# Lists of the experts' rows made between their products, in both expert-choice stages of a transformer kernel

## The chip, the cores and the metric

One NeuronCore of a Trainium2 chip runs the whole kernel. The metric is the device time of one execution in microseconds (us), lower is better. Engines are named as in the profile: PE (TensorE, matrix products), ACT (ScalarE), DVE (VectorE), POOL (GpSimd), SP (SyncE, which starts plain DMAs). PSUM is the memory that PE writes, SBUF the working memory.

## What is computed

Eight stages follow each other on a residual stream `x` of 16 × 512 tokens with 128 features in float32: attention, feed-forward, attention, feed-forward, and so on. The change concerns the sixth and the eighth stage, which both compute this ("expert choice"): each of 8 experts takes the k rows with the highest probability for it.

```python
x = x + _L1_ffn_ref(_layernorm(x, axis=-1), Ws, bs, W1, b1, W2, b2)

def _L1_ffn_ref(x, Ws, bs, W1, b1, W2, b2):
    B, S, D = x.shape                    # 16, 512, 128
    E = Ws.shape[1]                      # 8 experts, hidden size 512
    N = B * S                            # 8192 rows
    k = int(1.0 * N / E)                 # 1024 rows for each expert
    xf = x.reshape(N, D)
    route_prob = jax.nn.softmax(xf @ Ws + bs, axis=-1).T
    route_vals, routes = jax.lax.top_k(route_prob, k)
    xin = xf[routes]
    h = jax.nn.gelu(jnp.einsum('ekd,edf->ekf', xin, W1) + b1[:, None, :])
    out = jnp.einsum('ekf,efd->ekd', h, W2) + b2[:, None, :]
    out = out * route_vals[..., None]
    final = jnp.zeros((N, D), dtype=x.dtype).at[routes.reshape(-1)].add(out.reshape(-1, D))
    return final.reshape(B, S, D)
```

## The kernel before, in words

`X` lies in SBUF for the whole kernel as 64 tiles of 128 rows (16 blocks `b` of 4 tiles). The stages run one after the other; in every stage each engine has an instruction queue of its own, written out by hand, and waits on semaphores. `feed_forward` makes an expert-choice stage, with tensors named `..._choice_a` for the sixth stage and `..._choice_b` for the eighth. It has three blocks, and all engines meet at the end of each.

1. *Scores.* DVE takes the layernorm statistics of all 64 tiles (L1514, by `statistics`), then block by block normalises `xn` (L1524). PE turns the block (L1476), ACT copies it to `xt` (L1492), PE multiplies it by the router's weights (L1481) and DVE adds the router bias into `gate` (L1534). There is one `xt`, so PE's turn, ACT's copy and PE's product of a block follow each other. SP stores `X` and `xn` to DRAM as rows (`x_rows`, `xn_rows`).
2. *Choice.* Softmax on DVE and ACT. Then 30 steps of bisection on the bits of the probability find each expert's cut: DVE counts the probabilities above a candidate (L1700), PE adds up the counts of an expert's lines (L1580), DVE corrects the candidate in small operations on one column (L1703 to L1706, L1699). Prefix sums give each chosen row its place. Then each expert's list of 1024 row numbers and probabilities is made by a product: `entry` (L1755) holds for each token what the list is to hold, as bfloat16 parts, `onehot` (L1766) its place, 8 tiles at a time in two buffers, and PE multiplies them over 64 tiles into `small` (L1599). DVE takes from `small` the probabilities `prob` and the row numbers `ids` (L1775 to L1780). A loop does this for the 8 experts, and only then the block ends.
3. *Products.* POOL gathers an expert's 1024 rows from `xn_rows` by 8 indirect DMAs of 128 rows each, whose row numbers it reads from SBUF (`idx`, a copy of `ids`, L1931 and L1936). PE turns them (L1967), DVE copies them to `xgT` (L2017), PE multiplies by the first weights (L1979), ACT applies the gelu to `hid` (L2005), PE multiplies by the second weights and adds the bias (L1989, L1991) into `ybank`, DVE scales by `prob` into `yg` (L2023), and POOL adds the rows to `x_rows` by 8 indirect DMAs (L1945). POOL's own queue is: gather expert 0, gather expert 1, and then for each expert e scatter it in two halves, wait until it has landed, and gather expert e+2. At the end SP loads `x_rows` back into `X` (L1923).

The other two feed-forward stages (`pair_feed_forward`, tensors `..._top_a` and `..._top_b`) have their scores in another form, with two `xt` and statistics of 16 tiles at a time; their POOL also starts indirect DMAs (L2338, L2343). They aren't changed.

## Time and profile before

| | us |
|---|---|
| median of 3 runs (lowest, highest) | 6796.9 (6795.12, 6797.51) |
| the profiled execution | 6796.88 |
| its span, first to last instruction | 6795.0 |
| PE busy in the span | 5119.2 (75%) |
| DVE busy | 3765.0 (55%) |
| ACT busy | 3317.2 (49%) |
| POOL busy | 1198.3 (18%) |

The shares are means over eight stages with different limits, so they don't say what bounds the two stages that the change touches; these are to be read by stretches of the timeline. The sixth stage lies at about 3748 to 4335 us of the span and the eighth at about 6192 to 6779 us.

### The profile page before, as it was taken

The numbers are of one execution on the slowest core, as the hardware profiler recorded it, in microseconds if no ns is written. First come the engines' busy times: TensorE is split into PE (matmuls) and PEld (weight loads), VectorE is DVE, ScalarE is ACT, GpSimd is POOL, SyncE is SP. The second block draws the span as 40 slices with busy tenths as digits, with TensorE's granted clock in tenths as the row PEclk, the third lists the DMA queues.
The fourth block names the chain that finished last, engine by engine and source line by source line (L and its number), as shares of the span: only waits on it lengthen the run. The fifth ranks groups of instructions, "written<-read, shape, count | busy, mean of one in ns | idle before, by whom it ended". The sixth has DMA issues, their size and how long they took to land. (4 is left out here: it accounts for less than half of the span.)

```text
span 6795.0 us, 99022 instructions
## 1 busy us (share of the span) xinstructions
PE 5119.2 (75%) x30008; PEld 2655.2 (39%) x30008; DVE 3765.0 (55%) x7864; ACT 3317.2 (49%) x5089; POOL 1198.3 (18%) x1163
## 2 busy tenths in 40 slices
PE   5999619578888709678888347599999999996276
PEld 1333319434444409522222335334343434343244
DVE  4333435477777634566666571266667676755631
ACT  4888416345555315366767002366666666662011
POOL 1000043423333143311110006200000000000035
PEclk9999759789999759789999558799999999997567
DMA  3332511223232501222222103200000000001014
GB/s 82 77 77 75 76 32 50 62 67 89 84 89 85 92 25 51 75 69 60 59 59 54 52 0 53 59 1 0 0 0 0 0 0 0 0 0 52 0 33 91
DMA packets 298528, 310.99 MB, mean 46 GB/s; under 512 B 61526, under 2 KB 249142, under 8 KB 298180
## 3 DMA queue, kind: packets, MB, share of 16 engines
q1 hardware_dynamic: 265756, 269.55, 16.3%
q0 software_dynamic: 32448, 37.39, 2.8%
q8 instruction: 171, 2.80, 0.2%
q14 instruction: 153, 1.25, 0.1%
HBM read 193.61 MB, written 112.80 MB: 45 GB/s over the span
## 5 line engine op out<-in xcount | busy, mean ns | idle before, releaser
L953 ACT ACTIVATE prob_relative<-slot_relative 128x1024 f32<-128x1024 f32 x512 | 499.9, 1042 | 145.9 <-PE obank_relative L827 140.1
L2880 ACT ACTIVATE prob_wide<-slot_wide 128x1024 f32<-128x1024 f32 x512 | 493.8, 1016 | 149.7 <-PE slot_wide L2779 149.7
L1271 DVE TENSOR_TENSOR slot_decay<-slot_decay,dtab_decay 128x512 f32<-128x512 f32 (+3 forms) x1024 | 453.9, 494 | 166.0 <-PE slot_decay L787 146.3
L953 ACT ACTIVATE prob_rms<-slot_rms 128x1024 f32<-128x1024 f32 x512 | 498.0, 1040 | 85.2 <-PE slot_rms L802 83.3
L953 ACT ACTIVATE prob_decay<-slot_decay 128x640 f32<-128x640 f32 x512 | 358.7, 705 | 343.7 <-PE slot_decay L808 342.8
L2779 PE MATMUL slot_wide<-qT_wide,kT_wide 64*128 64x512 f32 x2048 | 508.9, 615 | 2.9 <-ACT prob_wide L2880 2.9
L1283 DVE TENSOR_TENSOR prob_relative<-prob_relative,rtab_relative 128x512 f32<-128x512 f32 (+1 forms) x512 | 409.9, 850 | 128.3 <-ACT prob_relative L953 119.0
L2792 PE MATMUL obank_wide<-prob_wide,v_wide 128*64 128x512 f32 x2048 | 467.7, 599 | 1.8 <-DVE zT_wide L2937 1.8
L1931 POOL COPY idx_choice_b<-ids_choice_b 128x8 int32 (+1 forms) x8 | 1.5, 189 | 2221.9 <-POOLq L1555 2209.9
L827 PE MATMUL obank_relative<-prob_relative,vaug_relative 128*32 128x512 f32 x2048 | 291.4, 644 | 116.7 <-DVE prob_relative L1283 115.0
L2923 DVE TENSOR_TENSOR sums_wide<-sums_wide,prob_wide 128x1024 f32<-128x1024 f32 x256 | 313.7, 1225 | 28.7 <-ACT prob_wide L2880 0.2
L2005 ACT ACT_TABLE_LOAD x8 | 10.3, 1283 | 652.7 <-PE hbank_choice_b L1979 326.4
L802 PE MATMUL slot_relative<-qst_relative,kst_relative 128*128 128x512 bf16 x1024 | 301.5, 393 | 34.4 <-ACT prob_relative L953 28.3
L802 PE MATMUL slot_rms<-qst_rms,kst_rms 128*128 128x512 bf16 x1024 | 283.8, 383 | 34.4 <-DVEq L1263 24.1
L2748 PE MATMUL bench_wide<-wT_wide,xnT_wide 128*128 128x512 f32 x512 | 264.9, 639 | 44.1 <-ACT sq_wide L2838 24.6
L827 PE MATMUL obank_rms<-prob_rms,vaug_rms 128*32 128x512 f32 x2048 | 272.6, 604 | 31.7 <-ACT prob_rms L953 31.6
L2779 PEld LDWEIGHTS slot_wide<-qT_wide,kT_wide 64*128 64x128 f32 x2048 | 176.4, 186 | 287.6 <-issue 280.6
L2853 ACT ACTIVATE rinv_wide<-rbank_wide 128x512 f32<-128x512 f32 x128 | 76.4, 597 | 409.5 <-PE rbank_wide L2803 409.5
L787 PE MATMUL slot_decay<-qst_decay,kin_decay 128*128 128x512 bf16 (+3 forms) x1024 | 229.6, 310 | 60.8 <-issue 41.5
L2792 PEld LDWEIGHTS obank_wide<-prob_wide,v_wide 128*64 128x64 f32 x2048 | 136.0, 137 | 317.8 <-issue 315.2
L802 PE MATMUL slot_decay<-qst_decay,kst_decay 128*128 128x512 bf16 (+3 forms) x1024 | 229.3, 307 | 32.5 <-DVE slot_decay L1271 30.7
L2923 DVE TENSOR_TENSOR sums_wide<-prob_wide 128x1024 f32<-128x1024 f32 x128 | 156.8, 1225 | 174.1 <-ACT prob_wide L2880 174.1
(756 smaller groups left out, 10632.2 us busy)
## 6 DMA issues: line engine op xcount, KB each, us to landing
scratch_decay<-parts_decay SPq DMA_DIRECT2D x192, 128.0 KB, 2.3
qst_rms<-scratch_rms SPq DMA_DIRECT2D x64, 288.0 KB
kst_rms<-scratch_rms SPq DMA_DIRECT2D x192, 96.0 KB
qst_relative<-scratch_relative SPq DMA_DIRECT2D x64, 288.0 KB
kst_relative<-scratch_relative SPq DMA_DIRECT2D x192, 96.0 KB
qst_decay<-scratch_decay SPq DMA_DIRECT2D x128, 128.0 KB
scratch_rms<-parts_rms SPq DMA_DIRECT2D x96, 128.0 KB, 2.3
kst_decay<-scratch_decay SPq DMA_DIRECT2D x192, 64.0 KB
```

What stands on the lines that cost most here:

```text
L787: last = nc.tensor.matmul(slot[:, u % 3, at:at + m], kin[:, h, kb * P:(kb + 1) * P], qst[:, h, q0:S], start=True, stop=False, skip_group_c ...
L802: last = nc.tensor.matmul(slot[:, u % 3, at:at + m], kst[:, h, kb * P:(kb + 1) * P], qst[:, h, q0:S], start=not decay, stop=not decay, ski ...
L827: last = nc.tensor.matmul(obank[32 * j:32 * j + 32, c0:c1], vaug[:, vp, kb, G * g + j, :], prob[:, Q % 2, j, at + c0 - q0:at + c1 - q0], s ...
L953: nc.scalar.activation(prob[:, Q % 2, j, 0:c1 - c0], slot[:, u % 3, c0:c1], ACT.Exp).then_inc(exp_done, 1)
L1271: last = nc.vector.tensor_tensor(sl, sl, dtab[:, h, 0:m], ALU.mult)
L1283: last = nc.vector.tensor_tensor(v, v, rtab[:, h:h + 2, c0:c0 + (hi - lo) * P], ALU.mult)
L2748: nc.tensor.matmul(bench[:, j % 2, :], xnT[:, t * P:(t + 1) * P], wT[:, j // 2, (j % 2) * S:(j % 2 + 1) * S], start=True, stop=True).then_ ...
L2779: last = nc.tensor.matmul(slot[:, u % 2, hh * S:(hh + 1) * S], kT[r, Q, kb * P:(kb + 1) * P], qT[r, Q, :], start=True, stop=True)
L2792: nc.tensor.matmul(obank[W * hh:W * hh + W, :], v[:, kb, (2 * Q + hh) * W:(2 * Q + hh + 1) * W], prob[:, Q % 2, kb, hh * S:(hh + 1) * S], ...
L2853: nc.scalar.activation(rinv[:], rbank[:], ACT.Ln).then_inc(r_logged, 1)
L2880: nc.scalar.activation(prob[:, Q % 2, u % 4, :], slot[:, u % 2, :], ACT.Exp).then_inc(exp_done, 1)
L2923: add = nc.vector.tensor_tensor(sums[:, Q % 2, :], first, prob[:, Q % 2, i + 1, :], ALU.add)
```

## The change

`model` calls a new function, `choice_feed_forward`, for the sixth and the eighth stage. It computes the same, in one block instead of three:

- Scores in the form of `pair_feed_forward`: statistics of 16 tiles at a time, all of `xn` kept, two `xt`, PE's product of block b−1 after the turn of block b.
- The bisection is written out 30 times without a loop, with three small operations on DVE instead of five.
- `row`, `lane` and the count constants are bfloat16, `fact` holds its five parts side by side, and `entry` is made for one expert at a time (two buffers). `onehot` holds 64 tiles in one buffer. DVE runs `mark(e)` (one `in_lane`, five `entry`, eight `onehot`) and `read(e)` for e = 0 to 7 as fast as its waits let it. PE makes lists 0 and 1 ahead of the products, and list e+2 between the first and the second product of expert e.
- ACT copies the turned rows and scales by `prob`, both of which DVE did.
- POOL reads `ids` directly, without the copy `idx`, and waits for the landing of scatter e−1 before scatter e instead of behind it.
- SP loads the weights of expert e when those of e−2 are used; `X` is loaded back by four DMAs instead of one.

```diff
+def choice_feed_forward(nc, sem, A, X, NB, w, uid):
...
+            @block.gpsimd
+            def _(pool):
+                def gather(e):
+                    pool.wait_ge(list_read, e + 1)
+                    if e >= 2:
+                        pool.wait_ge(xg_turned, 2 * (e - 1))
+                    for j in range(JT):
+                        nc.gpsimd.indirect_dma_start(
+                            xg[:, e % 2, j, :], None, xn_rows,
+                            bass.IndirectOffsetOnAxis(ap=ids[:, e, j:j + 1], axis=0)).then_inc(gathered[e % 2], 16)
+
+                def scatter(e):
+                    if e:
+                        pool.wait_ge(scattered, 16 * JT * e)
+                    for half in range(2):
+                        pool.wait_ge(yg_ready, 2 * e + half + 1)
+                        for j in range(HALF * half, HALF * (half + 1)):
+                            nc.gpsimd.indirect_dma_start(
+                                x_rows, bass.IndirectOffsetOnAxis(ap=ids[:, e, j:j + 1], axis=0),
+                                yg[:, e % 2, j, :], None, compute_op=ALU.add).then_inc(scattered, 16)
...
+                gather(0)
+                gather(1)
+                for e in range(E):
+                    scatter(e)
+                    if e + 2 < E:
+                        gather(e + 2)
...
+                def make_list(e):
+                    pe.wait_ge(entries, e + 1)
+                    if e >= 2:
+                        pe.wait_ge(list_read, e - 1)
+                    for i in range(T):
+                        if i % 8 == 0:
+                            pe.wait_ge(hot_ready, e * (T // 8) + i // 8 + 1)
+                        last = nc.tensor.matmul(small[:, 64 * (e % 2):64 * (e % 2) + LIST], onehot[:, i, :],
+                                                entry[:, e % 2, i, :], start=(i == 0), stop=(i == T - 1),
+                                                skip_group_check=True)
+                        if i % 8 == 7:
+                            last.then_inc(list_filled, 1)
...
+                    if e + 2 < E:
+                        make_list(e + 2)
...
+                    act.wait_ge(list_read, e + 1)
+                    for half in range(2):
+                        act.wait_ge(y_filled, 2 * e + half + 1)
+                        if e >= 2:
+                            act.wait_ge(scattered, 16 * JT * (e - 1))
+                        for j in range(HALF):
+                            at = HALF * half + j
+                            last = nc.scalar.activation(yg[:, u, at, :], ybank[:, half, j * D:(j + 1) * D], ACT.Copy,
+                                                        scale=prob[:, e, at:at + 1])
+                        last.then_inc(yg_ready, 1)
...
+                for i in range(BITS):
+                    nc.vector.tensor_scalar(work2[:], gate2[:], cand[R].bitcast(F32), None, ALU.is_ge, ALU.add,
+                                            accum_out=col[R, 0:1]).then_inc(counted, 1)
+                    dve.wait_ge(summed, i + 1)
+                    link(nc.vector.tensor_scalar(bit[R], small[R, 0:1], float(KEEP), float(1 << (BITS - 1 - i)),
+                                                 ALU.is_ge, ALU.mult))
+                    link(nc.vector.tensor_tensor(cur[R], cur[R], bit[R], ALU.bitwise_or))
+                    if i + 1 < BITS:
+                        link(nc.vector.tensor_scalar(cand[R], cur[R], 1 << (BITS - 2 - i), None, ALU.bitwise_or))
...
+                def mark(e):
+                    if e >= 2:
+                        dve.wait_ge(list_filled, (e - 1) * (T // 8))
+                    link(nc.vector.tensor_tensor(in_lane[:, e % 2], lane[:, e, :].unsqueeze(2).to_broadcast([P, T, JT]),
+                                                 lanes, ALU.is_equal))
+                    for k in range(FACTS):
+                        last = nc.vector.tensor_tensor(entry[:, e % 2, :, k * JT:(k + 1) * JT], in_lane[:, e % 2],
+                                                       fact[:, e, :, k].unsqueeze(2).to_broadcast([P, T, JT]), ALU.mult)
+                    last.then_inc(entries, 1)
+                    for g in range(T // 8):
+                        if e:
+                            dve.wait_ge(list_filled, (e - 1) * (T // 8) + g + 1)
+                        nc.vector.tensor_tensor(onehot[:, 8 * g:8 * g + 8, :], countb[:].unsqueeze(1).to_broadcast([P, 8, P]),
+                                                row[:, e, 8 * g:8 * g + 8].unsqueeze(2).to_broadcast([P, 8, P]),
+                                                ALU.is_equal).then_inc(hot_ready, 1)
...
+                mark(0)
+                read(0)
+                for e in range(1, E):
+                    mark(e)
+                    read(e)
...
-            lambda: feed_forward(nc, sem, A, X, "choice", NB, dict(
+            lambda: choice_feed_forward(nc, sem, A, X, NB, dict(
```

In the order of instructions, PE's queue of the changed kernel stands like this where the products begin; the first row is the lists of experts 0 and 1, and the rest is expert 0 up to the first of its second products.

```order
L2753 MATMUL small_choice_a<-entry_choice_a,onehot_choice_a 128x40 x128
L2768 MATMUL bench_choice_a<-ident_choice_a,xg_choice_a 128x128 x8
L2779 MATMUL hbank_choice_a<-xgT_choice_a,up_choice_a 128x512 x8
L2753 MATMUL small_choice_a<-entry_choice_a,onehot_choice_a 128x40 x64
L2792 MATMUL ybank_choice_a<-down_choice_a,hid_choice_a 128x128 x4
```

The 64 products of a list, which all stood ahead of the products before, now lie between an expert's first products (`hbank`) and its second (`ybank`).

On DVE, before, the entries of all experts were made at once and the lists by a loop in the block ahead of the products:

```order
L1755 TENSOR_TENSOR entry_choice_a<-in_lane_choice_a,fact_choice_a 128x512x8 x5
L1758 UNCONDITIONAL_BRANCH
L1758 ISA
L1766 ISA
L1766 TENSOR_TENSOR onehot_choice_a<-count_choice_a,row_choice_a 128x1024
```

Now the same queue holds, for each expert, this run (`part`, `row` and `ids` belong to `read`, the rest to `mark`):

```order
L2930 TENSOR_TENSOR in_lane_choice_a<-lane_choice_a,countb_choice_a 128x512
L2933 TENSOR_TENSOR entry_choice_a<-in_lane_choice_a,fact_choice_a 128x64x8 x5
L2939 TENSOR_TENSOR onehot_choice_a<-countb_choice_a,row_choice_a 128x1024 x8
L2947 COPY part_choice_a<-small_choice_a 128x8
L2948 TENSOR_TENSOR part_choice_a<-part_choice_a,small_choice_a 128x8
```

Fourteen operations with two inputs in SBUF follow each other for each expert, and nothing else of DVE's stands in the products any more. On POOL the loop is gone and the queue begins so:

```order
L2675 DMA xg_choice_a<-xn_rows_choice_a,ids_choice_a 128x128 x16
L2685 DMA x_rows_choice_a<-yg_choice_a,ids_choice_a 8192x128 x8
L2675 DMA xg_choice_a<-xn_rows_choice_a,ids_choice_a 128x128 x8
L2685 DMA x_rows_choice_a<-yg_choice_a,ids_choice_a 8192x128 x8
```

The sixteen gathers, the eight scatters of an expert and the eight gathers of the next but one follow each other as before; what is gone is the copy of the row numbers between them.

## Rows read from the trace of the kernel before

**Rows 1.** The sixth stage by stretches, all engines; the columns head the rows.

```profile
core 0: us, PE busy (x) PEld busy (x) DVE busy (x) ACT busy (x) POOL busy (x), PEclk, DMA share, GB/s
...
3844.00:3929.00 85.00, 17.56 (x60) 15.00 (x60) 46.35 (x211) 0.00 (x0) 0.00 (x0) 0.50 0.00 0
...
3954.00:3976.00 22.00, 0.00 (x0) 0.00 (x0) 21.97 (x6) 0.00 (x0) 0.00 (x0) 0.50 0.00 0
...
3976.00:4082.00 106.00, 69.90 (x512) 53.31 (x512) 81.61 (x105) 0.00 (x0) 0.17 (x1) 0.50 0.00 0
...
4082.00:4317.00 235.00, 176.88 (x832) 120.14 (x832) 29.98 (x88) 48.52 (x68) 163.00 (x136) 0.85 0.33 54
```

**Rows 2.** Timeline, scores of the fourth and the sixth stage (start, busy, idle before).

```profile
2316.01 3.18 DVE L183 BATCH_NORM_STATS2 stats_top_b<-X 128x6 f32<-128x128 f32 x16
...
2384.52 0.19 DVE L2378 TENSOR_TENSOR gate_top_b<-ybank_top_b,rb_top_b 128x32 f32<-128x32 f32 x1 [1.51 <-PE ybank_top_b L2182]
...
3756.22 12.46 DVE L183 BATCH_NORM_STATS2 stats_choice_a<-X 128x6 f32<-128x128 f32 x64
...
3836.86 0.69 DVE L1684 TENSOR_REDUCE tok_choice_a<-gate_choice_a 128x64 f32<-128x512 f32 x1 [0.62 <-PEq L1433]
```

**Rows 3.** Timeline of the bisection: its first memset, then one step.

```profile
3843.04 0.48 DVE L1693 MEMSET ones_choice_a<- 128x512 f32 x1 [0.17 <-DVE gate_choice_a L1630]
...
3903.79 0.75 DVE L1700 TENSOR_SCALAR_CACHE_REDUCE work_choice_a<-gate_choice_a,colT_choice_a 128x512 f32<-128x512 f32 x1
...
3905.23 0.16 DVE L1703 TENSOR_SCALAR colT_choice_a<-small_choice_a 128x1 int32<-128x1 f32 x1 [0.68 <-PE small_choice_a L1580]
...
3906.63 0.75 DVE L1700 TENSOR_SCALAR_CACHE_REDUCE work_choice_a<-gate_choice_a,colT_choice_a 128x512 f32<-128x512 f32 x1
```

**Rows 4.** Groups by line: count, busy us, mean ns, idle before.

```profile
L1755 DVE TENSOR_TENSOR entry_choice_a<-in_lane_choice_a,fact_choice_a 128x4096 bf16<-128x4096 bf16 x5 | 21.8, 4421 | 0.0
...
L1746 DVE TENSOR_TENSOR in_lane_choice_a<-lane_choice_a,count_choice_a 128x4096 bf16<-128x4096 f32 x1 | 4.4, 4426 | 0.0
...
L1766 DVE TENSOR_TENSOR onehot_choice_a<-count_choice_a,row_choice_a 128x1024 bf16<-128x1024 f32 x64 | 75.7, 1223 | 9.1 <-PE small_choice_a L1599 5.9 <-issue 3.2
...
L1599 PE MATMUL small_choice_a<-entry_choice_a,onehot_choice_a 128*128 x512 | 69.9, 212 | 67.8 <-DVE onehot_choice_a L1766 66.3 <-issue 0.2
...
L2305 ACT ACTIVATE part_top_a<-ybank_top_a,xg_top_a 128x128 f32<-128x128 f32 x91 | 33.4, 368 | 28.2 <-PE ybank_top_a L2250 28.2
```

**Rows 5.** Timeline of POOL from one expert's gathers to the next one's.

```profile
4130.37 0.19 POOL L1931 COPY idx_choice_a<-ids_choice_a 128x8 int32 x1 [2.00 <-DMA x_rows_choice_a<-yg_choice_a,idx_choice_a]
...
4135.30 0.95 POOL L1936 DMA_INDIRECT xg_choice_a<-xn_rows_choice_a,idx_choice_a  x1 [0.30 <-issue]
...
4154.72 1.56 POOL L1945 DMA_INDIRECT x_rows_choice_a<-yg_choice_a,idx_choice_a  x1 [0.30 <-issue]
...
4158.38 0.19 POOL L1931 COPY idx_choice_a<-ids_choice_a 128x8 int32 x1 [2.10 <-DMA x_rows_choice_a<-yg_choice_a,idx_choice_a]
```

**Rows 6.** Timeline of PE in the products of one expert.

```profile
4117.48 0.66 PE L1967 MATMUL bench_choice_a<-ident_choice_a,xg_choice_a 128*128 128x128 f32 x4
...
4120.04 7.03 PE L1979 MATMUL hbank_choice_a<-xgT_choice_a,up_choice_a 128*128 128x512 f32 x16
...
4138.41 0.48 PE L1991 MATMUL ybank_choice_a<-b_choice_a,ones_choice_a 1*128 x2
```

**Rows 7.** Timeline of DVE and POOL in the fourth stage, around its scatter.

```profile
2454.69 2.79 DVE L2483 TENSOR_TENSOR owner_top_b<-held_top_b,count_top_b 1x2548 f32<-1x2548 f32 x1
...
2455.59 2.78 POOL L2338 DMA_INDIRECT xg_rows_top_b<-xng_top_b,spots_top_b  x1 [210.04 <-DVE spots_top_b L2481]
...
2461.47 0.97 POOL L2338 DMA_INDIRECT xg_rows_top_b<-xng_top_b,spots_top_b  x1 [0.31 <-issue]
...
2463.87 8.88 DVE L2493 TENSOR_TENSOR X<-X,xng_top_b 128x2048 f32<-128x2048 f32 x4
...
2464.01 10.25 POOL L2338 DMA_INDIRECT xg_rows_top_b<-xng_top_b,spots_top_b  x1 [0.30 <-issue]
```

311 lines of the change are left out of this document (310 added, 1 removed).

## The prediction

> **What bounds the kernel now.** I read the sixth stage by windows first [rows 1], then the timelines inside each window, then the groups by line. In the windows the reader is to see a chain of stretches with a different owner each: 85 us of bisection in which DVE and PE are both under 55% busy, so that latencies set its pace; 22 us in which DVE alone makes the entries; 106 us of lists, DVE busy 81.6 of them; and 235 us of products, of which PE is busy 176.9 and POOL 163.0. No stretch overlaps the next. In the products the period of an expert is 28.0 us (4130.37 to 4158.38 [rows 5]), and it is POOL's: eight gathers of 0.95 + 0.30, eight scatters of 1.56 + 0.30, a copy, and some 2 us of waiting for the landing. PE needs 21.4 us for an expert (4117.48 to 4138.89 [rows 6]) and waits the rest. The eighth stage has the same form, and I count it as a second sixth.
>
> **The change part by part.** The sum is made against the profiled execution, 6796.88 us, which is also the median. All terms are for one stage.
>
> *Scores.* The new form is that of the fourth stage, which runs from its first statistics to its last `gate` in 68.7 us (2316.01 to 2384.71 [rows 2]); the sixth takes 80.0 (3756.22 to 3836.24). Taken: −11.3. No gain is excluded by the row itself; between 0 and −13.
>
> *Ends of blocks, setup.* One block boundary goes (0.62 [rows 2]) and memsets of about 0.48 move to where DVE waits for loads [rows 3]: −2.0, between −0.6 and −2.5.
>
> *Bisection.* A step takes 2.84 us (3903.79 to 3906.63 [rows 3]): 1.44 up to the first correction, then small operations and the loop's branch. With three operations of 0.16 + 0.03 a step is 1.44 + 0.57 = 2.01. Thirty steps fall from 84.7 (a little under 85.2) to 60.3: −24.4, between −18 (a step of 2.2) and −27.
>
> *Placing.* `in_lane` for all experts, 4.4 us [rows 4], leaves this phase; a copy and part of a wait for the second turn go, and the five strided writes of `fact` may each cost 0.2 more. Estimate −5.6, between −4 and −7. The parts so far come to 43.3.
>
> *Lists and products.* Before, from the first entry (3954) to the end of the products (4317) [rows 1] it is 363 us. For after I count from the start of `mark(0)`.
>
> DVE's run for one list: five entries an eighth as long as 4421 ns [rows 4], 0.55 + 0.06 each, 3.1 in all; `in_lane` 0.7; eight `onehot` of 1024 elements at the entries' 1.08 ns each, 1.11 + 0.03, so 9.1 (they took 1223 ns). Together 12.9. Behind it PE's last group takes 1.1 (69.9 us / 64 [rows 4]) and `read` about 1.1: list 0 is read at 15.2, the run of list 1 lies at 15.2 to 28.1, that of list 2 at 30.4 to 43.3. PE per expert: 21.4 + a list, 4.6 at the full clock (an estimate, half of 69.9/8 = 8.7 and a little) = 26.2. POOL per expert: 8 × 1.86 + 8 × 1.25 = 24.9. ACT's four scalings of 0.37 [rows 4] put 1.5 us between a half's products and its scatter; they and its two copies fit beside its 48.5 us of 235.
>
> What decides is whether POOL keeps its 24.9 when DVE runs lists beside it, which it never does in the products of before. The nearest case stands in [rows 7]. A DVE operation with both inputs in SBUF runs 2454.69 to 2457.48; POOL's indirect DMA begun at 2455.59 takes 2.78 and ends 0.89 behind it, where one beside other work takes 0.97. Four such operations follow each other for 8.88 us from 2463.87; the DMA begun at 2464.01 takes 10.25, to 2474.26. It did not get in between the four. Each of the fourteen operations of a list is of that kind. So I take it that a run holds up POOL from its start to its end, except that one DMA gets through behind `in_lane`, where the next operation waits for it. A run then costs POOL 12.9 − 1.5 = 11.4 us. The rule of the Trainium skill that bears on it ("SBUF — State Buffer", "SBUF: two separate sides") is that VectorE and GpSimd share an exclusive pair of ports which the one that starts first holds for its whole instruction, and a VectorE operation with two SBUF inputs takes it against a GpSimd one that reads SBUF. The first part agrees with the 2.78; but release at every instruction's end would have let POOL in between the four, and the 10.25 speaks against that. What it would be by the rule stands as a rival below.
>
> With that the stage runs so: gather 0 starts at 15.3, gets one DMA through behind `in_lane`, two between the runs, one more in the next run, and its last four behind 43.3: it ends at 48.3. PE starts at 50.3 (2.0 of landing, as [rows 5] show for the scatter). The first scatter starts 24.1 later, at 74.4: turn and first products 9.6 [rows 6] and 2.4 for a clock that has gone low in the wait, list 4.6, half of the second products 6.0, scaling 1.5. Then follow: a first period of 42.8 (24.9, the rest of the run of list 3, 6.5, and all of list 4's, 11.4); three of 24.9 + 11.4 = 36.4, for the runs of lists 5, 6 and 7; two without a run, 26.1 and 25.1; a scatter with its landing, 18.2, and the last, 17.2. The end is at 74.4 + 42.8 + 109.2 + 51.2 + 18.2 + 17.2 = 313. Against 363: −50. With a list on PE at the low clock (8.7) it is 317; with `onehot` at 1.22 and dearer ends of the held DMAs 321; the least is 308.
>
> The wait for scatter e−1 moved ahead of scatter e is free: the gathers lie between. SP's loads and the four-part load of `X` are left at nothing; the same bytes move.
>
> *Sum.* −11.3 − 2.0 − 24.4 − 5.6 − 50 = −93.3 for a stage, −187 for both: 6796.9 − 187 = **6610 us**. With each term at its bound it is 6575 to 6650, and taken together more likely 6590 to 6635.
>
> **The rivals.**
>
> *POOL gets in between operations.* For it: the 2.78 alone would read so. Against: the 10.25. If at every second boundary one DMA gets in, a run costs about 6 us, gather 0 ends at 32.3, and the first scatter starts at 58.4. Periods are 33.9, three of 31, then as above: 58.4 + 33.9 + 93 + 51.2 + 35.4 = 272, −91, a stage −134.3, both −269: 6528 us. This is also what the Trainium skill's rule would give.
>
> *POOL isn't held up at all.* For it: operands here are bfloat16 with repeated elements, those of [rows 7] were float32. Then PE sets the pace: it starts at 29.2, the first scatter at 51.4, and 51.4 + 5 × 26.2 + 25.1 + 35.4 = 243, −120, both stages −327: 6470 us.
>
> *Slower: PE's clock stays low.* The granted clock was 0.50 (1.2 GHz) through bisection and lists and 0.85 over the products [rows 1], where PE waits 6.6 us of 28.0. With waits of 10 us of 36.4 it may fall each time. If it stayed at 0.50 throughout, PE's work of an expert is 176.88/8 × 0.85/0.50 = 37.6, the list 8.7, pauses inside 3.7: 50 us. The end is at 50.3 + 6 × 50 + 2 × 41.3 + 11.3 = 444, +81, a stage +38: 6872 us. It decides from 45 us for an expert on. Against: PE would then be busy nearly without a pause, and in such work the clock did rise.
>
> *Dearer for POOL.* Each DMA under a run might hold up DVE in turn, or waits chain so that lists come late to PE. 330 or more for the part, 6650 or more in all.
>
> **How the numbers follow.** The forecast 0.66, POOL in between 0.15, POOL free 0.12, slower 0.03, dearer but still faster 0.04. The predicted time is the first's. The range takes it whole with its dear side and the second rival: 6515 to 6650; POOL free, the slower case and what lies above are left out. The forecast's own range is 6590 to 6635. 0.2% (14 us) is about what a measurement of this kernel can tell from no change. Faster 0.96: every case but the slower one and its like; within 0.2% 0.01; slower 0.03.
>
> **What would show it.** Scores of 68 to 69 us; bisection steps of 2.0; in each list's run one POOL DMA of 9 to 12 us that ends just behind the last `onehot`; scatter 1, 2 and 3 starting 36 us apart; PE waiting some 10 us for gathers of most experts. The forecast is wrong if POOL's DMAs beside `onehot` take 1 us (then 6470), or 2 to 3 us each (then 6528); if PE's turn follows the gathers by a clock of 0.50 through whole experts; or if `onehot` or `entry` take a length other than 1.1 and 0.6, which changes every run by eight or five times that. It is also wrong if DVE makes the lists later than PE wants them.

## The result

| | us |
|---|---|
| before, median | 6796.5 |
| after, median of 4 runs (lowest, highest) | 6510.5 (6506.6, 6514.9) |
| after / before, 95% interval | 0.9579 (0.9567, 0.9591) |
| span before, after | 6795.0, 6505.7 |

The change makes the kernel 286 us faster. The forecast was 187 us (6610 us), with a range down to 6515: the direction was right, and the time lies below the range. The stretches of the sixth stage in the changed kernel, as in [rows 1] (a view by windows; the columns head it):

```profile
core 0: us, PE busy (x) PEld busy (x) DVE busy (x) ACT busy (x) POOL busy (x), PEclk, DMA share, GB/s
3757.00:3826.00 69.00, 40.20 (x192) 39.49 (x192) 48.06 (x270) 9.38 (x16) 0.00 (x0) 0.50 0.48 138
3832.00:3892.00 60.00, 17.54 (x60) 14.97 (x60) 36.56 (x150) 0.00 (x0) 0.00 (x0) 0.50 0.00 0
3913.00:4175.00 262.00, 193.39 (x1344) 134.71 (x1344) 109.33 (x153) 72.64 (x145) 192.12 (x128) 0.83 0.29 45
```

The reader is to see that scores (69 us), bisection (60) and the rest are still separate stretches, but that lists and products are now one of 262 us, in which PE is busy 193 us and POOL 192. Beside the stretches of before this gives, for the sixth stage:

| part | before | after | difference | forecast |
|---|---|---|---|---|
| scores | 80.0 | 68.7 | −11.3 | −11.3 |
| setup, softmax and block end | | | −1.0 | −2.0 |
| bisection, 30 steps | 84.7 | 60.0 | −24.7 | −24.4 |
| placing | 25.4 | 21.3 | −4.1 | −5.6 |
| first entry to last landing | 363.0 | 261.6 | −101.4 | −50 |

The sum is −142.5, and the next stage begins 142.7 us earlier. So four of the five terms were right within 1.5 us, and for one the forecast was half of what came. DVE's timeline of the changed kernel, one step of the bisection, beside [rows 3]:

```profile
3847.95 0.74 DVE L2881 TENSOR_SCALAR_CACHE_REDUCE work_choice_a<-gate_choice_a,cand_choice_a 128x512 f32<-128x512 f32 x1
...
3849.96 0.75 DVE L2881 TENSOR_SCALAR_CACHE_REDUCE work_choice_a<-gate_choice_a,cand_choice_a 128x512 f32<-128x512 f32 x1
```

From one count to the next it is 2.01 us, as worked out ahead.

What the missing term consists of is seen on POOL and DVE. Below are two gathers of expert 0 and the first scatter, then the first scatters of experts 1 to 4, and last DVE's run of `onehot` beside the first of them (start, busy, idle before):

```profile
3935.85 1.96 POOL L2675 DMA_INDIRECT xg_choice_a<-xn_rows_choice_a,ids_choice_a  x1 [0.30 <-issue]
...
3940.39 0.95 POOL L2675 DMA_INDIRECT xg_choice_a<-xn_rows_choice_a,ids_choice_a  x1 [0.30 <-issue]
...
3964.99 7.90 POOL L2685 DMA_INDIRECT x_rows_choice_a<-yg_choice_a,ids_choice_a  x1 [8.09 <-ACT yg_choice_a L2829]
...
4000.29 1.62 POOL L2685 DMA_INDIRECT x_rows_choice_a<-yg_choice_a,ids_choice_a  x1 [0.30 <-issue]
...
4029.20 1.62 POOL L2685 DMA_INDIRECT x_rows_choice_a<-yg_choice_a,ids_choice_a  x1 [0.30 <-issue]
...
4058.83 1.62 POOL L2685 DMA_INDIRECT x_rows_choice_a<-yg_choice_a,ids_choice_a  x1 [0.30 <-issue]
...
4087.43 1.62 POOL L2685 DMA_INDIRECT x_rows_choice_a<-yg_choice_a,ids_choice_a  x1 [0.30 <-issue]
```

```profile
3931.24 9.16 DVE L2939 TENSOR_TENSOR onehot_choice_a<-countb_choice_a,row_choice_a 128x1024 bf16<-128x1024 bf16 x8
...
3962.22 9.16 DVE L2939 TENSOR_TENSOR onehot_choice_a<-countb_choice_a,row_choice_a 128x1024 bf16<-128x1024 bf16 x8
```

Beside the run that begins at 3931.24, each gather takes 1.97 us and starts 2.27 after the one before it: two operations of 1.14. Behind the run it takes 0.95. So POOL gets in between DVE's operations, which the sum of the forecast had ruled out. Gather 0 ends 29.4 us after the first mark at 3913.19 (forecast 48.3), the first scatter starts at 51.8 (74.4), and the scatters of experts 1 to 4 begin 28.6 to 29.6 us apart (36.4). Only one DMA of each stage is held in the way that was forecast: in this one the scatter of 3964.99 takes 7.90 us, to 1.5 us behind the end of the run that began at 3962.22.

PE in an expert of the changed kernel (compare [rows 6]):

```profile
4013.58 1.78 PE L2753 MATMUL small_choice_a<-entry_choice_a,onehot_choice_a 128*128 128x40 bf16 x64
...
4031.27 1.11 PE L2768 MATMUL bench_choice_a<-ident_choice_a,xg_choice_a 128*128 128x128 f32 x4 [4.00 <-DMA xg_choice_a<-xn_rows_choice_a,ids_choice_a]
```

The list, 64 products, takes 1.78 us at the full clock and not the 4.6 of the estimate. PE waits some 4 us for the gathers of most experts (9 once), and turn and part of the first products then run at the low clock, but it is up again before the second products.

### The profile page after: what moved, and what is told of

Same layout as the page of the kernel before. It is cut to its first block and busy times, and to the rows that moved or that the text cites. A ratio compares the mean times of both kernels' runs of the same rounds, so it can differ in the third digit from the quotient of the medians.

```text
span 6505.7 us, 95125 instructions
## 1 busy us (share of the span) xinstructions
PE 4965.4 (76%) x29755; PEld 2574.5 (40%) x30008; DVE 3701.5 (57%) x7740; ACT 3366.0 (52%) x5243; POOL 1256.0 (19%) x1147
## 5 line engine op out<-in xcount | busy, mean ns | idle before, releaser
L2675 POOL DMA_INDIRECT xg_choice_b<-xn_rows_choice_b,ids_choice_b x64 | 85.4, 1334 | 2072.6 <-DVE ids_choice_b L2951 2053.4
L802 PE MATMUL slot_relative<-qst_relative,kst_relative 128*128 128x512 bf16 x946 | 281.0, 390 | 50.3 <-ACT prob_relative L953 35.7
L802 PE MATMUL slot_rms<-qst_rms,kst_rms 128*128 128x512 bf16 x945 | 268.6, 382 | 42.2 <-issue 24.7
L787 PE MATMUL slot_decay<-qst_decay,kin_decay 128*128 128x128 bf16 (+3 forms) x960 | 214.0, 303 | 69.6 <-issue 41.8
L3354 DVE TENSOR_TENSOR rfix_wide<-rbank_wide,rinv_wide 128x512 f32<-128x512 f32 x128 | 88.5, 692 | 247.2 <-ACT rinv_wide L3275 247.2
```

Of the source, the lines that this page charges most:

```text
L787: last = nc.tensor.matmul(slot[:, u % 3, at:at + m], kin[:, h, kb * P:(kb + 1) * P], qst[:, h, q0:S], start=True, stop=False, skip_group_c ...
L802: last = nc.tensor.matmul(slot[:, u % 3, at:at + m], kst[:, h, kb * P:(kb + 1) * P], qst[:, h, q0:S], start=not decay, stop=not decay, ski ...
L2675: nc.gpsimd.indirect_dma_start(xg[:, e % 2, j, :], None, xn_rows, bass.IndirectOffsetOnAxis(ap=ids[:, e, j:j + 1], axis=0)).then_inc(gathe ...
```

## The experiments

The theories after the result. **A**: POOL's DMA needs what a two-input DVE operation holds once, and gets it at the end of an operation. **B**: gathers get in, scatters don't. **C**: the first DMA after a pause is held. **D**: two inputs have nothing to do with it. Times of the variants are given as their ratio to the runs of before on the same chip, times 6796.5.

### The cost by itself: probe

A kernel of its own, in which nothing of the model is computed: DVE runs operations of one kind while POOL issues 8 indirect DMAs. Its figures, and those of the other small kernels below, are of one execution.

```python
ARMS = [("gather", "none", 0), ("scatter", "none", 0), ("store", "none", 0),
        ("gather", "onehot", 14), ("scatter", "onehot", 14), ("store", "onehot", 14),
        ("gather", "entry", 24), ("scatter", "entry", 24),
        ("gather", "wide", 7), ("scatter", "wide", 7),
        ("gather", "scalar", 64), ("scatter", "scalar", 64),
        ("gather", "psum", 14), ("scatter", "psum", 14),
        ("gather", "onehot_late", 14), ("scatter", "onehot_late", 14)]
```

> Nothing of the model is computed here: sixteen arms one after the other, each 8 indirect DMAs of 128 rows on POOL (gather from DRAM, scatter with addition, or plain store) beside a run of DVE operations (none; onehot of 128x1024 bfloat16 with two SBUF inputs; entry of 128x512; 128x2048 float32 of 2.2 us; onehot for one tile at a time with one SBUF input; onehot with one input in PSUM; onehot begun when the first DMA has landed). Theory A (every boundary between DVE operations is a chance, whatever the DMA): beside onehot a gather and a scatter both take about 2.3 us with their gap, beside the 2.2 us operations about 4.5 or 2.2. Theory B (the kind of DMA decides): gathers beside onehot take 2.0 us each, but the first scatter is held to the end of the run, some 14 us, and so is a plain store or not, which tells whether the addition or the SBUF source matters. Theory C (the first DMA after a pause is held, whatever its kind): the first gather beside onehot takes some 14 us, and in the arms begun late no scatter does. Theory D (nothing to do with two inputs in SBUF): the arms with one SBUF input or a PSUM input look like those with two. With A, B or C those arms show 0.95 for a gather and 1.55 for a scatter.

POOL's timeline, a DMA out of the middle of an arm: gather and scatter beside `onehot`; gather beside 128x2048 operations, beside one-input operations, and beside those with an input in PSUM:

```profile
84.61 1.97 POOL L307 DMA_INDIRECT xg_probe<-x_rows_probe,ids_probe  x1 [0.30 <-issue]
...
103.69 1.97 POOL L309 DMA_INDIRECT x_rows_probe<-xg_probe,ids_probe  x1 [0.31 <-issue]
...
175.50 1.90 POOL L307 DMA_INDIRECT xg_probe<-x_rows_probe,ids_probe  x1 [0.30 <-issue]
...
208.57 0.94 POOL L307 DMA_INDIRECT xg_probe<-x_rows_probe,ids_probe  x1 [0.30 <-issue]
...
239.74 0.94 POOL L307 DMA_INDIRECT xg_probe<-x_rows_probe,ids_probe  x1 [0.30 <-issue]
```

| beside | gather | scatter | store |
|---|---|---|---|
| nothing | 0.94 | 1.54 | 0.96 |
| `onehot`, 1.14 us | 1.97 | 1.97 | 1.97 |
| entries, 0.61 us: the first three | 1.3 to 1.5 | 1.9 to 2.1 | |
| entries: the last five | 0.94 | 1.54 | |
| 2048 columns float32, 2.2 us | 1.90 | 1.90 | |
| one SBUF input, 0.16 us | 0.94 to 0.99 | 1.55 | |
| one input in PSUM, 1.14 us | 0.94 | 1.54 to 1.62 | |

A DMA waits for the next end of an operation and ends 0.9 us (gather) or 1.5 us (scatter) behind it. With the gap of 0.30, gathers and scatters beside `onehot` start 2.27 us apart, two operations of 1.14, and beside the long ones 2.20, one operation of 2.2. Beside entries the fourth gather began within 0.01 us of an operation's start and got through at once, and so did those behind it. A holds, B falls (scatters get in as gathers do), C falls (no first DMA was held), and D falls: with one input, or one of the two in PSUM, nothing is lost. This is the rule of the Trainium skill ("SBUF — State Buffer", "SBUF: two separate sides") as it was cited ahead, and for DVE's side the trace agrees, with release at the end of each instruction. For POOL's side it doesn't: by the rule a DMA that comes first would hold DVE up for its whole 0.94 us, but beside entries the operation behind such a start followed after 0.65 us and not 0.60. So POOL holds up DVE for some 0.05 us only.

### Does a certain place in an operation hold the DMA: probe_phase

Also a kernel of its own. An ACT copy of growing width starts two DMAs at ten places in an operation of the run, about 0.16 us apart.

> Nothing of the model is computed here. Twenty arms: a run of twelve onehot operations on DVE (1.14 us each), and two indirect DMAs on POOL after a pause, begun at ten places about 0.1 us apart within an operation; ten arms with gathers, ten with scatters. In the changed kernel the first scatter of a stage was issued 0.48 us after such an operation had begun and took 7.9 us, to the end of the run. Theory of the place: a DMA issued near that place in an operation misses all boundaries; so one or two of the ten scatters take some 9 us, the others 1.6 to 2.7, and perhaps so for the gathers. Theory of bad luck by kind or of another cause (what POOL did before, or the waits between the operations): no DMA here takes more than 2.7 us, and all end about 0.9 us (gather) or 1.5 us (scatter) behind a boundary.

```profile
39.82 2.14 POOL L271 DMA_INDIRECT xg_probe<-x_rows_probe,ids_probe  x1 [39.38 <-ACT line_probe L261]
...
137.08 0.94 POOL L271 DMA_INDIRECT xg_probe<-x_rows_probe,ids_probe  x1 [10.54 <-ACT line_probe L261]
...
191.16 2.52 POOL L273 DMA_INDIRECT x_rows_probe<-xg_probe,ids_probe  x1 [10.08 <-ACT line_probe L261]
```

The first gather takes 2.14, 1.91, and so on down to 0.94, where an operation's end is just reached, and then 1.92 again; the first scatter 1.55 to 2.52. It is a wait for the next end, whatever the place, and none of the 20 first DMAs was held longer. So the place alone doesn't explain the 7.90.

### Lists ahead of the products: lists_ahead

```diff
-                make_list(0)
-                make_list(1)
+                for e in range(E):
+                    make_list(e)
...
-                    if e + 2 < E:
-                        make_list(e + 2)
```

> All eight lists ahead of the products again, the rest as changed. If DVE's runs are what lengthens POOL's period (29.0 us for an expert against 24.9 by its own durations), the period is 25 us here: the lists end 8 x 14.3 = 114 us after the first mark, the first scatter starts at about 135, six periods of 25 and 35 for the last two scatters end at 320, against 262 now: 59 us more for a stage, 6629 us in all. If something else in the changed stage makes the 29.0, it stays, and the time is 6680 us.

Measured: ratio 0.9747 (0.9731, 0.9764), 6625 us, where 6629 was expected. Gathers of successive experts on POOL:

```profile
4137.23 1.01 POOL L2675 DMA_INDIRECT xg_choice_a<-xn_rows_choice_a,ids_choice_a  x1 [0.30 <-issue]
...
4162.32 1.01 POOL L2675 DMA_INDIRECT xg_choice_a<-xn_rows_choice_a,ids_choice_a  x1 [0.30 <-issue]
```

The period is 25.1 us, so the 4 us by which it was longer are DVE's runs. Of the 286 us, the interleaving is worth 115 (6625 − 6510); the rest is in the other edits.

### One SBUF input: one_input

```diff
-        row = sb("row", [P, E, T], BF16)
+        row = sb("row", [P, E, T])
...
-                        nc.vector.tensor_tensor(onehot[:, 8 * g:8 * g + 8, :], countb[:].unsqueeze(1).to_broadcast([P, 8, P]),
-                                                row[:, e, 8 * g:8 * g + 8].unsqueeze(2).to_broadcast([P, 8, P]),
-                                                ALU.is_equal).then_inc(hot_ready, 1)
+                        for i in range(8 * g, 8 * g + 8):
+                            last = nc.vector.tensor_scalar(onehot[:, i, :], countb[:], row[:, e, i:i + 1], None,
+                                                           ALU.is_equal)
+                        last.then_inc(hot_ready, 1)
```

> onehot is made one tile at a time by an operation with one SBUF input and a value for each partition; entries are as before. Theories A, B and C, in which two SBUF inputs take the port that POOL needs: gathers beside onehot fall from 1.97 to 0.95 us, gather 0 ends after 10 us, the period is POOL's own 25 us, and the part from the first mark to the last landing falls from 262 to about 234 us: 6455 us in all. Theory D: the gathers beside onehot stay at 1.97, and the time stays at 6510 us. If 64 small operations take DVE much longer than the 9.2 us of the 8 (over 0.3 us each), lists come late and the gain is lost: 6510 to 6560 us.

Measured: 0.9740 (0.9707, 0.9773), 6620 us, 110 us slower than the changed kernel, a miss by 165. The gathers did what was expected:

```profile
3933.70 0.96 POOL L2675 DMA_INDIRECT xg_choice_a<-xn_rows_choice_a,ids_choice_a  x1 [0.30 <-issue]
...
3968.47 1.63 POOL L2685 DMA_INDIRECT x_rows_choice_a<-yg_choice_a,ids_choice_a  x1 [15.47 <-ACT yg_choice_a L2829]
...
4008.38 1.62 POOL L2685 DMA_INDIRECT x_rows_choice_a<-yg_choice_a,ids_choice_a  x1 [11.85 <-ACT yg_choice_a L2829]
```

0.96 us, but the scatters then wait 12 to 15 us for `yg`. Behind that stands PE. By a window of one expert, and PE's timeline of the list and what follows:

```profile
core 0: us, PE busy (x) PEld busy (x) DVE busy (x) ACT busy (x) POOL busy (x), PEclk, DMA share, GB/s
...
3968.00:4008.00 40.00, 35.54 (x173) 26.00 (x172) 14.29 (x71) 9.04 (x19) 20.17 (x16) 0.63 0.25 40
```

```profile
3988.62 1.81 PE L2753 MATMUL small_choice_a<-entry_choice_a,onehot_choice_a 128*128 128x40 bf16 x53
...
3992.35 0.27 PE L2753 MATMUL small_choice_a<-entry_choice_a,onehot_choice_a 128*128 128x40 bf16 x4 [0.53 <-issue]
3993.79 0.23 PE L2753 MATMUL small_choice_a<-entry_choice_a,onehot_choice_a 128*128 128x40 bf16 x2 [1.17 <-issue]
...
3998.12 2.06 PE L2792 MATMUL ybank_choice_a<-down_choice_a,hid_choice_a 128*128 128x128 f32 x8 [0.16 <-issue]
```

An expert takes 40 us, PE is busy 35.5 of them, and the granted clock is 0.63. The list ends in gaps of 0.5 to 1.2 us that no engine releases, and behind them eight second products take 2.06 to 2.08 us and not 1.16: the low of the two clock levels (1.2 GHz). DVE stood idle beside these gaps (from 3972.83 to 3998.37), so its small operations don't make them. This is the forecast's slower rival, PE at a low clock for most of an expert (there 50 us), and it came in a variant that was to be faster. What it needs is not POOL's hold but a list in which PE stands still.

### Runs beside scatters: beside_scatter

The landing of an expert's first scatter gets a semaphore of its own, and DVE waits for it.

```diff
+                    if e >= 3:
+                        dve.wait_ge(began, 16 * (e - 2))
                     link(nc.vector.tensor_tensor(in_lane[:, e % 2], ...
```

> DVE begins the run of list e (from e = 3) only when the first of the scatters of expert e-3 has landed, so that it lies beside scatters and not beside gathers. Theory B (a scatter is held through the whole run): one scatter of each expert takes some 12 us, 7 us more than the gathers lose now, five times in a stage: 6580 us. Theory A: scatters get in between operations, lose 0.4 us each, and the time falls to about 6490 us. Theory C: POOL doesn't pause there, so no scatter is held: as A.

Measured: 0.9651 (0.9635, 0.9667), 6559 us, near the 6580 of theory B, and B is false all the same:

```profile
3975.20 1.97 POOL L2688 DMA_INDIRECT x_rows_choice_a<-yg_choice_a,ids_choice_a  x1 [0.31 <-issue]
...
4029.29 1.62 POOL L2688 DMA_INDIRECT x_rows_choice_a<-yg_choice_a,ids_choice_a  x1 [10.43 <-ACT yg_choice_a L2834]
...
4039.62 1.75 POOL L2688 DMA_INDIRECT x_rows_choice_a<-yg_choice_a,ids_choice_a  x1 [2.85 <-ACT yg_choice_a L2834]
...
4121.45 8.26 POOL L2688 DMA_INDIRECT x_rows_choice_a<-yg_choice_a,ids_choice_a  x1 [2.63 <-ACT yg_choice_a L2834]
```

```profile
core 0: us, PE busy (x) PEld busy (x) DVE busy (x) ACT busy (x) POOL busy (x), PEclk, DMA share, GB/s
...
4029.00:4071.00 42.00, 36.55 (x171) 25.95 (x169) 13.69 (x19) 8.85 (x18) 21.45 (x16) 0.62 0.23 38
```

Scatters beside the run take 1.97 as gathers do. The time went where it went in one_input: 42 us for an expert at a clock of 0.62, after lists that had gaps. A list that waited for DVE for 1.25 us in all left the clock up. One scatter of each stage was held here as well, 8.26 us (4121.45) and 7.50. It is the first after a pause, but so is that of 4039.62, beside the same kind of run, with 1.75 us.

### The list in eight portions: two_spread and one_spread

```diff
                             last = nc.tensor.matmul(y, ones[0:1, 0:P], b2[:, e * D:(e + 1) * D], start=False,
                                                     stop=True, skip_group_check=True)
-                        last.then_inc(y_filled, 1)
+                            if j == HALF - 1:
+                                last.then_inc(y_filled, 1)
+                            if e + 2 < E:
+                                make_list(e + 2, [HALF * half + j])
```

one_spread has this with the one-input `onehot`, two_spread with the changed kernel's.

> The changed kernel, but the 64 products of list e+2 lie in eight portions between the eight groups of the second products of expert e. POOL sets the period (29.0 us, 4.1 of it beside onehot), so PE's order shouldn't matter by itself; DVE's run begins up to 12 us later and lies beside scatters, which lose 0.4 us each and not 1.0: some 1.7 us an expert less, 10 a stage: 6490 us. If the clock of PE falls less, PE's wait is longer and nothing is gained by it. If the list read later delays gather e+2, 6510 to 6530 us.

> onehot with one SBUF input as in the run one_input, and the list in eight portions as in two_spread. One_input took 40 us for an expert, all of them PE's, with PE's clock at 0.62 and stretches within the list in which PE stood still. Theory F or G, the stop or the weak work of the list brings the clock down: spread out it doesn't, PE takes 23.5 us, POOL 24.9 sets the period, and the part from the first mark to the last landing is about 235 us: 6455 us in all. If it is something else about the 512 small operations of DVE (their instructions, or the time they take) that slows PE, it stays near 6620 us.

Measured: two_spread 0.9540 (0.9524, 0.9556), 6484 us; one_spread 0.9514 (0.9499, 0.9530), 6466 us. Both expectations hold within 0.2% (6490 and 6455). one_spread on POOL, the first scatters of two experts, and by windows:

```profile
3988.43 1.62 POOL L2685 DMA_INDIRECT x_rows_choice_a<-yg_choice_a,ids_choice_a  x1 [0.30 <-issue]
...
4013.90 1.62 POOL L2685 DMA_INDIRECT x_rows_choice_a<-yg_choice_a,ids_choice_a  x1 [0.30 <-issue]
```

```profile
core 0: us, PE busy (x) PEld busy (x) DVE busy (x) ACT busy (x) POOL busy (x), PEclk, DMA share, GB/s
...
4000.00:4029.00 29.00, 25.62 (x188) 18.18 (x186) 21.73 (x115) 9.65 (x19) 23.73 (x18) 0.88 0.39 60
4029.00:4059.00 30.00, 29.08 (x252) 22.12 (x249) 15.60 (x77) 9.99 (x22) 23.91 (x21) 1.00 0.38 62
```

The period is 25.5 us, POOL's own 24.9 and a little, at a clock of 0.88 to 1.00. One_input and one_spread differ only in where the 64 products stand: 154 us. The share of the two-input `onehot` alone is the difference of two_spread and one_spread, 18 us by the ratios, whose intervals overlap slightly. It is clear of noise all the same: both ran on one chip, and there the four times of each (6478 to 6489 and 6465 to 6469 us) stand apart, with medians 14 us from each other. one_spread is the fastest version here, 44 us below the changed kernel.

### What stops PE in the list: probe_fetch, probe_far and one_hold

The gaps in one_input and beside_scatter stood in lists beside which POOL gathered; a list beside scatters had none. The theory (F) was that PE's instructions come late beside gathers.

> Nothing of the model is computed here. Arms on PE: 16 products of 128x512 in float32, then 64 small bfloat16 products as in a list, then 40 products of 128x128 in float32; beside them 16 indirect DMAs of POOL (gather, scatter, store), eight plain DMAs, or nothing; in two arms the small ones are spread over the last 40, in one PE pauses for some 4 us behind the list. Theory F (PE's instructions come late beside gathers): the list takes 1.8 us beside nothing and 4 us or more beside gathers, with idle stretches that no engine releases; scatters or plain DMAs may do it too. Theory G (the list itself, short products, makes PE's clock fall): no gaps anywhere, and the last 40 products fall to the low clock in all arms but the spread ones. Behind gaps of 2 us in all I expect the last 40 products at the low clock (0.26 us each) for some us, else 0.14.

> Nothing of the model is computed here. As in probe_fetch, no gap came into a list of 64 beside any DMA; but the rows gathered there lay in order, and the gaps in the runs one_input and beside_scatter began after some 48 small products. So here the list is 256 small products and the rows lie 61 rows apart (one arm has them in order). Theory F2 (PE's instructions come late beside gathers, seen only when what is fetched ahead is used up): 256 products take 6.8 us beside nothing, and 15 us or more beside gathers, in gaps of 0.5 to 1.2 us, and the clock falls behind them. If 256 take 6.8 us in all arms, gathers alone don't do it. If they gap beside nothing too, the rate of PE's instructions alone limits a long list.

Both are kernels of their own. PE's timeline beside gathers, of 64 products in order of rows, and of 256 with rows far apart, each with the products of 128x128 behind them:

```profile
88.54 1.78 PE L290 MATMUL small_probe<-entry_probe,hot_probe 128*128 128x40 bf16 x64
90.17 9.18 PE L307 MATMUL ybank_probe<-X,wt_probe 128*128 128x128 f32 x80
```

```profile
96.61 6.66 PE L290 MATMUL small_probe<-entry_probe,hot_probe 128*128 128x40 bf16 x256
103.12 9.18 PE L307 MATMUL ybank_probe<-X,wt_probe 128*128 128x128 f32 x80
```

The list takes 1.78 us beside gathers and beside nothing, and 256 take 6.66 in all arms; the 80 records behind them take 9.18 at the full clock. F falls in this form, and so does G, that such a list brings down the clock by itself. In the arm with a pause of 3.69 us ahead of them they took 10.82.

So the same was asked in the kernel. one_hold is one_input with one more wait on POOL:

```diff
                     pool.wait_ge(list_read, e + 1)
+                    if 2 <= e < E - 1:
+                        pool.wait_ge(list_filled, (e + 2) * (T // 8))
```

> As one_input, but gather e waits until list e+1 is complete, so that no gather runs while PE makes a list; nothing else is changed. Theory F2: the list has no gaps, PE keeps its clock in the second products, an expert takes 25 to 28 us and not 40, and the time falls from 6642 to about 6480 us although POOL has more to wait for. Rival (the list as one block brings the clock down by itself, or the 512 small operations of DVE do): gaps or the low clock stay, and so do 40 us for an expert and 6620 to 6660 us.

Measured: 0.9555 (0.9539, 0.9571), 6494 us, 126 below one_input, where 6480 was expected. The first two rows are of the list that is made before the held gathers begin and of what follows it; the other two are lists with the gathers held:

```profile
3957.57 0.37 PE L2755 MATMUL small_choice_a<-entry_choice_a,onehot_choice_a 128*128 128x40 bf16 x8 [0.93 <-DVE onehot_choice_a L2942]
...
3963.16 2.08 PE L2794 MATMUL ybank_choice_a<-down_choice_a,hid_choice_a 128*128 128x128 f32 x8
...
4016.06 1.78 PE L2755 MATMUL small_choice_a<-entry_choice_a,onehot_choice_a 128*128 128x40 bf16 x64
...
4045.73 1.78 PE L2755 MATMUL small_choice_a<-entry_choice_a,onehot_choice_a 128*128 128x40 bf16 x64
```

```profile
core 0: us, PE busy (x) PEld busy (x) DVE busy (x) ACT busy (x) POOL busy (x), PEclk, DMA share, GB/s
...
3996.00:4022.00 26.00, 24.38 (x188) 17.88 (x188) 17.79 (x81) 8.95 (x18) 21.12 (x17) 1.00 0.37 62
4022.00:4050.00 28.00, 23.42 (x159) 15.73 (x158) 13.53 (x73) 8.95 (x18) 20.86 (x18) 0.82 0.35 57
```

With no gather beside it the list takes 1.78 us without a gap, an expert 26 to 28 us, and the clock is 0.82 to 1.00. So within this stage it is the gathers beside the list that stop PE. That the stop brings the clock down, whoever makes it, is seen in the first of these lists: it waits for DVE three times for 0.93 us, and the second products behind it take 2.08 us as in one_input. By themselves, in small programs, gathers and a list don't make gaps, and neither do gathers beside the portions of eight in one_spread. What else is needed, whether the other transfers or the length of the program, stays open.

## Why the prediction was wrong

- *Scores, ends of blocks, bisection, placing*: right, −41.1 together against −43.3. The memsets that were moved did not vanish behind a load (0.9 us), and the five strided writes of `fact` took 0.88 us each and not 0.43, where 0.2 more was allowed. The bounds of the terms, as they stand, add up to 6588 and 6668 us and not to 6575 and 6650; the measured time is below both.
- *POOL held up by a run*: this is the step that failed: "So I take it that a run holds up POOL from its start to its end". It rested on one row, the 10.25 us of [rows 7]. Probe, probe_phase and the changed kernel show in its place that a DMA waits for the next end of an operation, costing about 1 us for a gather beside `onehot`, 0.4 for a scatter, and little beside entries. An expert lost 4 us and not 11.4. In the stage the forecast was 22.6 us too late with the first scatter and 29.6 too long in the four periods behind it, and 0.8 too short at the end: together the 51.4 us that the term is off. Not all of the 22.6 is POOL's: gather 0 ends 18.9 us sooner, and of the other 3.7 the list on PE is 2.8 (1.78 us and not 4.6).
- The trace of before had a row against this step, between those that [rows 7] show:

```profile
2457.52 2.80 DVE L2485 TENSOR_TENSOR owner_top_b<-owner_top_b,pairs_top_b 1x2548 f32<-1x2548 f32 x1
...
2458.68 2.48 POOL L2338 DMA_INDIRECT xg_rows_top_b<-xng_top_b,spots_top_b  x1 [0.30 <-issue]
```

  The DMA begun at 2455.59 [rows 7] ended at 2458.38, when the next operation with two inputs had begun at 2457.52: it got in between the two. The DMA behind it ended 0.84 us behind the end of that second operation. Two DMAs followed the right mechanism and one, the 10.25, didn't.
- The rival *POOL gets in between operations*, 6528 us, was the right mechanism, with the pitch of one DMA for two operations. It was 18 us too slow, since it let entries cost as much as `onehot` and took the list for 4.6 us; that it came so near is in part luck, since it had no DMA held for the rest of a run, 6 us a stage the other way. It had a chance of 0.15: the 2.78 of [rows 7] spoke for it, and one row against it was given too much weight.
- *POOL isn't held up at all*: wrong, but its bound was reached by one_spread, 6466 us against 6470.
- *PE's clock stays low*: not so in the changed kernel, where from the second expert on a list falls beside scatters, because POOL sets the pace: PE starts an expert about 2 us behind the end of its gathers, and its list comes 12 us later, at the end of the 15 us of the scatters. (The first list in the products lies beside the end of two gathers and had no gap.) This is a coincidence of phases. In one_input and beside_scatter it was lost, and an expert took 40 to 42 us.
- *What the 10.25 us are*, and the 7.90 of the changed kernel, stays open. Both end just behind DVE's run, so I take them for the same thing, which isn't shown; it is neither the kind of the DMA, nor the place in the operation, nor a pause alone. It costs some 6 us in each stage; lists_ahead, one_input, one_hold and both spread versions have none in these two stages.

## What to carry to other kernels

An estimate of contention should come from the rows of both kinds that the trace has, not from the longest. In these runs what a DMA of POOL loses beside DVE is set by where DVE's operations with two SBUF inputs end, so shorter ones (entries), or ones with a single SBUF input, give it back. An order on PE that puts a block of short products between long ones works only as long as nothing stops that block: spread out in portions it had no gap here, and the clock stayed up.

## What was not expected of the hardware

- Beside gathers PE stood still in a list of small products in gaps of up to 1.17 us without any engine to wait for, in the stage (one_input, beside_scatter) but not by itself.
- Stops in a list of 1.9 to 4.7 us in all cost some 12 us more behind them: eight second products went from 1.16 to 2.08 us and stayed so up to the next expert.
- DVE loses next to nothing when POOL gets in: eight `onehot` take 9.16 us with no DMA beside them (list 0) and 9.16 and 9.21 with them (lists 1 and 2).
- Now and then one DMA is held to the end of a run of two-input operations, 7.5 to 10.25 us, once in a stage.
